# Five waiting scatters of edge sums moved from the start of the norm stage to the end of the aggregation

## The reference, cut to what matters

```python
def _hconv(x, src, dst, ew, w1, b1, w2, b2, g, b):
    h = jax.nn.relu(x @ w1 + b1)
    msg = ew[:, None] * h[src]
    agg = jax.ops.segment_sum(msg, dst, num_segments=x.shape[0])
    h = agg @ w2 + b2
    return jax.nn.relu(_bn(h, g, b))
...
h = _hconv(x, src, dst, hyperedge_weight, c1_w1, c1_b1, c1_w2, c1_b2, c1_g, c1_b)
h = jax.nn.relu(_bn(h, bn1_g, bn1_b))
h = _hconv(h, src, dst, hyperedge_weight, c2_w1, c2_b1, c2_w2, c2_b2, c2_g, c2_b)
h = _bn(h, bn2_g, bn2_b)
```

```python
edge_proj = edge_attr @ W_sum + b_sum
sum3d = jax.ops.segment_sum(edge_proj, src, num_segments=num_nodes)
```

## Time and profile before

| | us |
|---|---|
| median of 3 runs | 5942.16 |
| lowest and highest of them | 5932.99, 5949.23 |
| the profiled execution | 5931.77 |
| its span, first to last instruction | 5930.0 |
| stage a1 (from the first gather to the barrier) | 442.8 to 1498.5 |
| stage n1 | 1499.9 to 1601.4 |
| stage rc | 1601.6 to 1743.8 |
| stage a2 | 1745.1 to 2796.4 |
| stage n2 | 2799.2 to 2900.8 |

### The profile page before, as it was taken

One profiled execution on the slowest core, in us unless ns is written; L12 is line 12 of the kernel. 1 busy time (PEld: TensorE's weight loads), 2 busy tenths in 40 slices (PEclk: granted clock), 3 DMA queues, 4 the chain that ended last, 5 costly groups with the idle time before them and its releaser, 6 DMA issues. The chain is left out here.

```text
span 5930.0 us, 77150 instructions
## 1 busy us (share of the span) xinstructions
PE 3471.5 (59%) x19263; PEld 3033.3 (51%) x19263; DVE 2787.4 (47%) x7703; ACT 2340.6 (39%) x6709; POOL 4321.1 (73%) x3891
## 2 busy tenths in 40 slices
PE   5655555555655555555555059978779946173503
PEld 4555555555445555555355048866558745162402
DVE  5545555555425555554688675535460202011026
ACT  2217666666336666665433023333442211021102
POOL 4887777777777777777788667875777777777763
PEclk7757778788778888777776579989989977586756
DMA  8765333333563333333688647768653212121415
GB/s 243 146 118 195 105 105 105 104 105 105 100 138 105 105 105 104 104 105 94 112 162 160 177 118 169 164 124 244 128 120 86 68 33 56 15 61 40 121 30 175
DMA packets 701853, 690.18 MB, mean 116 GB/s; under 512 B 98498, under 2 KB 622828, under 8 KB 700908
## 3 DMA queue, kind: packets, MB, share of 16 engines
q0 software_dynamic: 254944, 323.26, 27.8%
q1 hardware_dynamic: 432956, 339.38, 18.8%
q10 hardware_dynamic: 13776, 25.54, 1.2%
HBM read 484.11 MB, written 203.71 MB: 116 GB/s over the span
## 5 line engine op out<-in xcount | busy, mean ns | idle before, releaser
L698 POOL DMA_INDIRECT a_msg<-h_d,a_idx x1664 | 1578.8, 949 | 523.3 <-issue 465.5
L744 PE MATMUL a_part<-a_pick,a_msg 128*128 128x128 f32 x6656 | 1158.3, 342 | 872.7 <-DMA a_msg<-h_d,a_idx 684.8
L594 POOL DMA_INDIRECT sums_d<-ss_total,ss_row_i x784 | 1284.8, 1639 | 396.9 <-issue 276.4
L744 PEld LDWEIGHTS a_part<-a_pick,a_msg 128*128 128x128 f32 x6656 | 1057.1, 248 | 961.1 <-DVE a_pick L711 777.8
L3500 POOL DMA_INDIRECT es_edge<-gat_rows_d,el_idx x1024 | 988.7, 965 | 332.7 <-issue 293.9
L724 DVE TENSOR_TENSOR acc<-acc,a_part 128x256 f32 x1664 | 700.7, 421 | 950.4 <-PE a_part L744 792.8
L711 DVE TENSOR_SCALAR a_pick<-ramp,conv_rel,conv_weight 128x128 f32<-128x128 f32 x1680 | 631.7, 377 | 0.3
L2493 PE MATMUL e_yp<-cb_lent 128*128 128x256 f32 (+1 forms) x1568 | 360.0, 386 | 413.5 <-ACTq L2457 413.5
L2493 PEld LDWEIGHTS e_yp<-cb_lent 128*128 128x128 f32 (+1 forms) x1568 | 303.2, 194 | 458.3 <-ACTq L2457 415.1
L2481 PE MATMUL e_hp<-cb_lent 128*128 128x256 f32 (+1 forms) x1600 | 353.1, 376 | 16.9 <-DMA cb_lent<-in_L_ffn_W 16.9
L2455 ACT ACTIVATE cb_lent<-e_hp,e_b1c 128x256 f32<-128x256 f32 (+1 forms) x400 | 155.0, 470 | 480.2 <-PE e_hp L2481 479.3
(11 more groups left out here) (515 smaller groups left out, 6166.9 us busy)
## 6 DMA issues: line engine op xcount, KB each, us to landing
ss_key_row<-keys_d SPq DMA_DIRECT2D x98, 512.0 KB, 5.7
ss_pay<-in_edge_attr SPq DMA_DIRECT2D x97, 512.0 KB, 6.2
a_msg<-h_d,a_idx POOLq DMA_INDIRECT x1664, 2.7
experts_d<-cb_lent SPq DMA_DIRECT2D x96, 256.0 KB
es_edge<-gat_rows_d,el_idx POOLq DMA_INDIRECT x1024
cb_lent<-experts_d SPq DMA_DIRECT2D x29, 512.0 KB, 4.6
y_rows_d<-node_h SPq DMA_DIRECT2D x28, 512.0 KB
e_xs<-y_rows_d SPq DMA_DIRECT2D x56, 256.0 KB
```

The lines of the kernel that those rows point to most:

```text
L594: nc.gpsimd.indirect_dma_start(self.out_d[q], bass.IndirectOffsetOnAxis(ap=self.row_i[n % 4][:, j:j + 1], axis=0), self.total[n % 4][:, j, ...
L698: nc.gpsimd.indirect_dma_start(msg[(h % 2) * K + b][:], None, table, bass.IndirectOffsetOnAxis(ap=idx[h][:, b:b + 1], axis=0)).then_inc(ga ...
L744: mm = nc.tensor.matmul(part[b % BANKS][:, half, :], msg[(h % 2) * K + b][:, half * P:(half + 1) * P], pick[b][:], start=True, stop=True)
```

## The change

`EdgeSums.scatter` is split: its loop becomes `scatter_chunks`, which takes chunk numbers in place of group numbers. `aggregate` gets `sums` and `first_chunk`, and GpSimd scatters five chunks (`AGG_CHUNKS`) of the first waiting group behind its last gather, ahead of the barrier. `dense_and_norms` begins with that group's sixth chunk, so that it scatters 43 chunks in place of 48. Both aggregations do this. The stages rc and mg are served as before, and all 784 scatters are still made in the same order.

```diff
     def scatter(self, pool, first, last):
 
+        self.scatter_chunks(pool, max(first, 0) * self.B, last * self.B)
+
+    def scatter_chunks(self, pool, first, last):
+
         nc, B, Q = self.nc, self.B, self.Q
-        for chunk in range(max(first, 0) * B, last * B):
+        for chunk in range(first, last):
...
             over_windows(pool, W, window)
+            sums.scatter_chunks(pool, first_chunk, first_chunk + AGG_CHUNKS)
...
+AGG_CHUNKS = 5
...
-            sums.scatter(pool, first - 2, first + DENSE_GROUPS - 2)
+            sums.scatter_chunks(pool, (first - 2) * sums.B + AGG_CHUNKS, (first + DENSE_GROUPS - 2) * sums.B)
...
-            aggregate(k, "a1", h_d, src_i, rel, weight, conv_tile_row, acc, counts, 0,
-                      ClearRows(k, c2, "yr", y_rows_d, node_h))
+            aggregate(k, "a1", h_d, src_i, rel, weight, conv_tile_row, acc, counts, 0,
+                      sums, (at - 2) * sums.B, ClearRows(k, c2, "yr", y_rows_d, node_h))
...
             aggregate(k, "a2", h_d, src_i, rel, weight, conv_tile_row, acc, counts,
-                      CountBeside.BATCHES // 2)
+                      CountBeside.BATCHES // 2, sums, (at - 2) * sums.B)
```

More of the change, by code:

```diff
@@ L629, in _, with aggregate @@
             nc.vector.tensor_tensor(start[:], tile_start[:], within[:], ALU.add)
-def aggregate(k, tag, table, src_i, rel, weight, first_row, acc, counts, first_batch, clear=None):
+def aggregate(k, tag, table, src_i, rel, weight, first_row, acc, counts, first_batch, sums, first_chunk,
+              clear=None):
     nc = k.nc
```

## The result

| | us |
|---|---|
| kernel before, median of 7 runs | 5940.97 (5932.99 to 5949.23) |
| changed kernel, median of 7 runs | 5959.77 (5956.15 to 5965.35) |
| ratio, 95% interval | 1.0034 (1.0025 to 1.0044) |
| profiled execution after, its span | 5959.77, 5958.0 |

The account below looks back on a forecast made before the run. GpSimd's own DRAIN was taken to hold the barrier at the ends of a1 and a2. Aggregations and norm stages summed to 5.5 + 5.5 + 0 + 0 = +11.0 us, giving 5953.2 us, range 5944 to 5965.

Parts of the forecast that it names:

- The reading of the barrier: Ends of a1 and a2: GpSimd's DRAIN arrives last, by 0.9 and 2.2 us, so its idle time is a wait.
- The scatters' own cost: Ends of a1 and a2: five scatters at 1.86 us each add 9.3 us, 9.8 as upper bound.
- the lag: Recorded end of the last transfer to DRAIN's end: 4.7 us behind the fifth scatter, where gathers left 8.55.
- the first rival: Ends of a1 and a2: scatters come on top of the whole lag, +18.6 to +19.6 us; chance 0.15.
- The point at which it was to decide: Behind the fifth scatter: above a lag of 8.1 us the slowdown exceeds 17.8 us and can be told from no change.
- its own mark for a wrong forecast: Ends of a1 and a2: forecast wrong if the drain ends within 10 us of the last gather or over 17 behind.
- The argument against that rival: Ends of a1 and a2: lag depends on the last transfer's kind, and scatters leave 9.3 us for the gathers' remainder.
- The rival of hidden scatters: Ends of a1 and a2: the wait runs on during the scatters, +0.8 us a stage, +1.6 in all; chance 0.10.
- The norm stages: n1 and n2: five fewer scatters only lengthen GpSimd's first wait for rows; gain 0, at most 0.3 us a stage.
- the prediction's mark of over 1 us: n1 and n2: the forecast is wrong if a norm stage becomes over 1 us shorter.
- the lag that stays: Ends of a1 and a2: scatters add to an unshortened lag, +19.6 us at the range's high end; chance 0.15.
- the forecast's own mechanism: Ends of a1 and a2: scatters plus a shortened lag make each aggregation 5.5 us longer, +11.0 us; chance 0.70.

Follow-up runs that it names:

- late drain: Kernel before, with a wait for TensorE's last sum, a drain, then unused extra gathers (4 in a1, 20 in a2) at each aggregation's end: 5991.95 us.
- the run of earlier rows: Kernel before, with the norm stages' rows of the third and fourth group chosen at blocks 5 and 10, not 6 and 11: 5928.76 us against 5932.93.
- second and third groups: Later sets of runs, compared only within each set, in which the unchanged kernel before had medians of 6677.99 and 6667.71 us.
- the run with the wait: Changed kernel, with a drain ahead of a1's five scatters and a wait for TensorE's last sum ahead of a2's: 5964.47 us.

## Why the prediction came out as it did

**The reading of the barrier was right.** GpSimd's idle time at the end of the aggregations was its own DRAIN and not free. Five scatters delayed GpSimd's DRAIN by 9.86 us at each place, and the aggregations became 11.5 and 10.9 us longer.

**The scatters' own cost was right.** 9.3 us were taken for five; from the last gather's recorded end to the last scatter's it was 9.45 us.

**The failed step is the lag.** The prediction took 4.7 us behind the fifth scatter, and 8.96 us was measured, in both aggregations. The reason given was that what is drained is the same kind of work as in rc. That is not so: the kind of the last transfer does not set the length, what was issued ahead of it since the last drain does. Behind a drained queue five scatters leave 2.14 us; behind 832 gathers they leave 8.96. The row at the end of n1 showed 4.0 us because 48 transfers stand behind the drain ahead of it: 52 gathers leave 4.3. At the ends of rc and mg it is 72 and 200 scatters, with 4.7 and 5.4; the number does not explain these two by itself (see the last section). With the measured lag the prediction's own sum gives 2 x (9.45 + 8.96 - 8.55) = +19.7 us, and +18.8 was measured between medians. So the first rival came true. The point at which it was to decide, a lag of 8.1 us, was passed (the prediction's 2 x (9.3 + 8.1 - 8.55) is 17.7, not 17.8, which changes nothing), and so was its own mark for a wrong forecast, a drain that ends over 17 us behind the last gather: it ended 18.4 us behind.

**The argument against that rival failed on its second half too.** It said that five scatters leave 9.3 us for the gathers' remainder to finish. The late drain shows that the gathers leave nothing that time alone would finish: 8.546 us when the DRAIN begins 5.4 us later, where the lag is 8.55 without a pause. The Trainium skill, in "Perfetto Trace Analysis", section "Sequencer-only Instruction (DRAIN, etc)", puts the reported start of such an instruction where its semaphore waits are over. The late drain agrees, since its row starts at 1494.5, when TensorE's last sum, for which it waits, ends. But the row of the barrier's DRAIN starts at 1492.6, when the second of the five scatters was just ending, so its start in a row says nothing of when the work before it was done. Its end does.

**The rival of hidden scatters is excluded**, by 18.4 us from the last gather to the release where it needed about 9.3.

**The norm stages were right.** The forecast was a first wait of about 12.7 us and a second still of 3.35; they were 13.46 and 3.35. The extra 0.7 us is VectorE's, whose last step on the rows starts at 1542.61, 33.9 us behind the stage's first parameter load (1508.70) where it had been 33.2. From that load to the barrier n1 took 102.3 us, and 101.5 were forecast. One norm stage came out 0.8 us longer and the other 1.02 us shorter, which just touches the prediction's mark of over 1 us. Norm stages in the other runs, with 40 to 48 scatters and rows chosen as before, lie between 100.4 and 102.7, with no order by that number, so no part of the 18.8 us is put down to them. With GpSimd relieved further, the run of earlier rows showed that ScalarE and SyncE end the stage within 1.7 us of it.

**The range held the time, and that is owed to a rival.** Its high end was the lag that stays; the forecast's own mechanism gives 11.0 us, and its upper bound 13.3. No change that can be told was forecast, and slower by over 0.3%, to which 0.17 was given, is what the ratio of 1.0034 shows. The chances did not put it well: the lag that stays had 0.15, though two of the five rows on lags, and the only two behind gathers, already showed 8.55.

**What stays open.** The runs show that the length of the DRAIN comes from what was issued ahead of it, not what GpSimd does in it. They don't explain the step between five and six scatters, nor why 98 transfers can cost as much as 832 and 232 next to nothing, as the last section shows. Why an unchanged aggregation took 1276 us in the second and third groups was not looked into.

## What to carry to other kernels

Idle time of an engine ahead of a barrier is free only if the engine's own DRAIN is not what the barrier waits for; look at the barrier's line, see whose DRAIN ends last, and what lies between the last transfer and its end. Do not size the drain behind a new last instruction by a stage that happens to end with the same instruction: measure what the transfers ahead of it leave, and put new work on top of that at its full pace. Here a DRAIN behind up to 52 transfers could be sized by their number, one behind hundreds could not. Deferred work gained here, by some 10 of 6670 us, when it was moved out of a stage in which its engine hardly pauses into one in which it had waited for others, after that wait had been made short; the move without that was not tried.

## What the runs showed of the hardware

GpSimd's DRAIN behind indirect transfers costs time of its own, and at the same place of the program it is nearly the same in every run:

| issued since the last drain | end of the last transfer's record to the end of the DRAIN, us |
|---|---|
| 5 scatters | 2.14 |
| 13 gathers | 2.3 to 2.45, once 3.75 |
| 40 to 48 scatters | 3.4 to 4.1 |
| 52 gathers | 4.3, once 5.4 |
| 69 to 72 scatters | 4.55 to 4.8 |
| 184 scatters (input stage) | 4.8 to 5.0 |
| 200 scatters | 5.4 to 5.6 |
| 832 gathers | 8.55 |
| nothing | 0.05 |

By the transfers' own records the last packets landed 1.3 to 3.0 us behind the end of the last record in these cases, so from 40 scatters on, landing is not what sets the length. And the 8.55 us are spent even when all transfers have long landed.

From 40 to 52 transfers the shortest lags grow by 0.08 us with each (3.36 at 40, 3.58 at 43, 3.98 at 48, 4.23 at 51, 4.30 at 52), the same 0.08 that each of up to five scatters adds behind 832 gathers. But the number does not give the length beyond that. The kernel before has three later stages in which GpSimd's DRAIN begins when its last transfer's record is over, so that its own length can be read, behind 98, 232 and 1,025 indirect transfers:

```profile
L2012 POOLq DRAIN  x1: 8055/8055/8055, 3461.9 to 3461.9; - x1
...
L2131 POOLq DRAIN  x1: 695/695/695, 3978.1 to 3978.1; - x1
...
L2328 POOLq DRAIN  x1: 5281/5281/5281, 5763.3 to 5763.3; - x1
```

They begin 4.85, 2.07 and 1.67 us behind the last record, and in all thirteen traces they take 8.06, 0.70 and 5.28 us within 0.01. So 98 transfers cost nearly what 832 gathers do (0.08 us each), and 232 scatters a twelfth of it. The 232 come with pauses of GpSimd between them, the last one 4.76 us ahead of the last eight, and 0.695 us is what eight would cost at 0.08 us each; that the pauses let it work the others off is a guess, and a pause by itself did not do it in the run with the wait, where 7.46 us took nothing off.
